# At most two indirect DMAs in flight, on two alternating semaphores

## What is computed

```python
# L0: two GCN layers of width 64 and 128
h = h @ W;  agg = segment_sum(h[src] * norm[:, None], dst);  out = agg + b
# L1: mean of the neighbours
aggregated = segment_sum(x[src], dst) / degree;  out = relu((aggregated + x) @ W.T + b)
# L2: five layers with edge attributes
m = relu(h[src] + edge_attr);  agg = segment_sum(m, dst);  z = h + agg   # then an MLP and batch norms
# L3: two layers of attention, 4 heads of 32
alpha = sum(q[dst] * (k[src] + e)) / sqrt(32);  w = softmax over the edges of one dst
out = segment_sum((v[src] + e) * w, dst) + x @ Ws + bs
```

## Time and profile before

| | us |
|---|---|
| median of 3 runs | 11942.19 |
| lowest, highest run | 11933.62, 11957.39 |
| span of the profiled execution | 11940.9 |
| POOL busy (share) | 5772.2 (48%) |
| PE busy (share) | 7779.4 (65%) |
| DVE busy, ACT busy | 5508.8, 4782.2 |
| L1960 gathers busy, 2682 and 894 | 2587.9, 861.3 |
| L1214 gathers busy, 1664 | 1651.9 |

### The profile page before, as it was taken

How to read it: one execution, slowest core, us unless ns; L and a number is a source line. 1 busy time by engine, 2 the same in 40 slices (tenths; PEclk the granted TensorE clock), 3 DMA queues, 4 the chain that set the end, 5 groups by cost and what they waited for, 6 DMA issues and landing times. The chain is left out here.

```text
span 11940.9 us, 256001 instructions
## 1 busy us (share of the span) xinstructions
PE 7779.4 (65%) x61807; PEld 6543.1 (55%) x61808; DVE 5508.8 (46%) x14938; ACT 4782.2 (40%) x13040; POOL 5772.2 (48%) x5856
## 2 busy tenths in 40 slices
PE   5357757767767776776777777677645555455555
PEld 3345535547746675665665667576444444344454
DVE  6545533333334444445445444444535456445447
ACT  0023323332324435444444443444445555345554
POOL 2455555554455444443443443444255555465554
PEclk6568878868878887888888888788766778667777
DMA  2235532233335544544554544455344454344453
GB/s 53 66 109 146 149 87 80 81 111 94 92 90 155 150 143 130 152 150 121 156 151 120 155 150 135 139 155 152 102 130 144 146 146 131 106 142 146 143 148 105
DMA packets 1224489, 1511.30 MB, mean 127 GB/s; under 512 B 206846, under 2 KB 806434, under 8 KB 1207895
## 3 DMA queue, kind: packets, MB, share of 16 engines
q1 hardware_dynamic: 1016374, 1055.75, 28.2%
q0 software_dynamic: 207712, 450.99, 14.9%
HBM read 1276.37 MB, written 229.67 MB: 126 GB/s over the span
## 5 line engine op out<-in xcount | busy, mean ns | idle before, releaser
L1960 POOL DMA_INDIRECT rings<-rows_key,pick x2682 | 2587.9, 965 | 3112.8 <-ACT pick L1975 2447.1
L2091 PE MATMUL wide<-bigDEF,bigC 128*128 128x128 bf16 (+2 forms) x32256 | 2353.5, 233 | 1289.3 <-issue 1239.5
L2091 PEld LDWEIGHTS wide<-bigDEF,bigC 128*128 128x128 bf16 x32256 | 2044.1, 110 | 1614.9 <-issue 1560.1
L1214 POOL DMA_INDIRECT bigDEF<-rows_key_value,idx x1664 | 1651.9, 993 | 1372.9 <-ACT idx L1226 742.8
L2202 DVE TENSOR_TENSOR bigDEF<-bigDEF,part 128x128 f32 (+1 forms) x3576 | 1016.7, 284 | 2643.3 <-PE part L2056 1435.5
L1975 ACT COPY pick<-pairs 128x3 int32 (+1 forms) x1192 | 222.5, 189 | 3794.2 <-PE part L2056 2957.9
L2056 PE MATMUL part<-rings 128*128 128x128 f32 (+1 forms) x7152 | 1283.6, 323 | 469.5 <-issue 231.4
L2056 PEld LDWEIGHTS part<-rings 128*128 128x128 f32 (+1 forms) x7152 | 1095.2, 213 | 565.8 <-issue 487.4
L1960 POOL DMA_INDIRECT rings<-rows_hidden,pick x894 | 861.3, 963 | 757.0 <-ACT pick L1975 535.3
L1330 PE MATMUL part<-bigB,rings 128*128 x3328 | 739.0, 390 | 730.4 <-DVE bigDEF L1417 363.6
L1982 ACT ACTIVATE rings<-iota,pairs 128x128 f32<-128x128 f32 x3576 | 1173.1, 391 | 47.8 <-remote 34.8
(11 more groups left out here) (424 smaller groups left out, 10607.0 us busy)
## 6 DMA issues: line engine op xcount, KB each, us to landing
bigC<-sheaf_hots SPq DMA_DIRECT2D x1152, 256.0 KB
rings<-in_attr SPq DMA_DIRECT2D x2235, 64.0 KB
bigC<-sheaf_attr SPq DMA_DIRECT2D x120, 1024.0 KB
walk_value<-bigDEF SPq DMA_DIRECT2D x416, 256.0 KB
rings<-walk_value SPq DMA_DIRECT2D x416, 256.0 KB
rings<-sheaf_steps SPq DMA_DIRECT2D x192, 256.0 KB
sheaf_hots<-bigC SPq DMA_DIRECT2D x192, 256.0 KB
bigB<-sheaf_hots SPq DMA_DIRECT2D x192, 256.0 KB
```

Of the source, the lines that this page charges most:

```text
L1214: e.indirect_dma_start(gbuf[:, g, r, :], None, table, bass.IndirectOffsetOnAxis(ap=c.idx[:, g, r:r + 1], axis=0)).then_inc(c.gathered[g].s ...
L1960: e.indirect_dma_start(gbuf[:, draw(n), r, 0:width], None, table, bass.IndirectOffsetOnAxis(ap=c.pick[:, draw(n), r:r + 1], axis=0)).then_ ...
L2091: last = e.matmul(to, hot, terms, start=x < LOT and x % batch == 0 and j == 2, stop=x >= MARCH - LOT, skip_group_check=True)
```

## The change

Every gather but the first two of a block waits until the second last gather has landed. For this the semaphores per buffer become two that alternate from gather to gather (`ALOFT` = 2; three in the first preparation, where three lists are fetched in turn). Whoever consumed a buffer now waits on both semaphores, up to the count at the end of its bunch or group. The first round of `_converse` on POOL is taken out of the loop. Nothing is computed differently, and no transfer is added or removed.

```diff
+ALOFT = 2
-    c.fetched = [gate(f"fetched{i}", 0) for i in range(SHELVES)]
+    c.fetched = [gate(f"fetched{i}", 0) for i in range(ALOFT)]
-    c.drawing = [gate(f"drawing{i}", 0) for i in range(DRAWS)]
+    c.drawing = [gate(f"drawing{i}", 0) for i in range(ALOFT)]
-    c.gathered = [gate(f"gathered{i}", 0) for i in range(RING)]
+    c.gathered = [gate(f"gathered{i}", 0) for i in range(3)]
...
+                    if k > 0:
+                        e.wait_ge(c.gathered[t].sem, c.gathered[t].at(16 * k))
                     e.indirect_dma_start(out, None, ins[src],
...
@@ _fetch
-        at = first + k * size + a
+        at, done = first + k * size + a, (k * size + a) // ALOFT
+        landing = c.fetched[a % ALOFT]
+        if done > 0:
+            e.wait_ge(landing.sem, landing.at(16 * done))
         e.indirect_dma_start(shelves[b][:, a, :], None, c.attr,
-                             bass.IndirectOffsetOnAxis(ap=c.edgeS[:, at:at + 1], axis=0)).then_inc(c.fetched[b].sem, 16)
+                             bass.IndirectOffsetOnAxis(ap=c.edgeS[:, at:at + 1], axis=0)).then_inc(landing.sem, 16)
@@ _stow
-        e.wait_ge(c.fetched[b].sem, c.fetched[b].at(16 * size * (use + 1)))
+        for landing in c.fetched:
+            e.wait_ge(landing.sem, landing.at(16 * size // ALOFT * (k + 1)))
@@ _converse, store on SP and multiply on DVE
-                e.wait_ge(c.gathered[g].sem, c.gathered[g].at(16 * GROUP * (i + 1)))
+                for landing in c.drawing:
+                    _hold(e, landing, 16 * GROUP // ALOFT * (i * RING + g + 1), c.tick_dve)
@@ _converse on POOL
-            with _loop(e, 0, ROUNDS) as i:
+            def fetch(i, g):
+                _hold(e, c.index, i * RING + g + 1, c.tick_pool)
+                for r in range(GROUP):
+                    landing, done = c.drawing[r % ALOFT], (i * RING + g) * (GROUP // ALOFT) + r // ALOFT
+                    if not (isinstance(done, int) and done == 0):
+                        _hold(e, landing, done * 16, c.tick_pool)
+                    e.indirect_dma_start(gbuf[:, g, r, :], None, table,
+                                         bass.IndirectOffsetOnAxis(ap=c.idx[:, g, r:r + 1], axis=0)
+                                         ).then_inc(landing.sem, 16)
+            for g in range(RING):
+                fetch(0, g)
+            with _loop(e, 1, ROUNDS) as i:
                 for g in range(RING):
-                    _hold(e, c.index, i * RING + g + 1, c.tick_pool)
-                    for r in range(GROUP):
-                        e.indirect_dma_start(gbuf[:, g, r, :], None, table,
-                                             bass.IndirectOffsetOnAxis(ap=c.idx[:, g, r:r + 1], axis=0)
-                                             ).then_inc(c.gathered[g].sem, 16)
+                    fetch(i, g)
@@ _mixed on POOL, inside fetch(i, n)
+                    t = (LEAD + n) * BUNCH + r
+                    landing, done = c.drawing[t % ALOFT], i * (BODY * BUNCH // ALOFT) + t // ALOFT
+                    if not (isinstance(done, int) and done == 0):
+                        _hold(e, landing, done * 16, c.tick_pool)
@@ _mixed, scatter on PE (sum); the same in join on DVE (edge)
-                    _hold(e, c.drawing[draw(n)], uses(i, n, DRAWS), c.tick_pe)
+                    for b, landing in enumerate(c.drawing):
+                        _hold(e, landing, landed(i, n, b), c.tick_pe)
```

23 lines of the change are left out of this document (15 added, 8 removed).

## The result

| | before | changed |
|---|---|---|
| median, us (4 runs each) | 11949.79 | 12346.12 |
| lowest, highest | 11933.62, 11959.39 | 12330.54, 12357.03 |
| span of the profiled execution | 11940.9 | 12328.7 |

The changed kernel takes 1.0332 times as long (95% interval 1.0316 to 1.0348). The forecast was 12300 us, between 11960 and 12600.

A forecast was written before the change was run, and what follows sets the result against it. It took POOL to have thin room, idling mostly for ACT's indices, and to become the bound in `_converse` under the limit. 312 + 46 + 65 + 15 + 20 - 100 = +358 on 11942 gave 12300 us, range 11960 to 12600.

The forecast's parts named there:

- `_converse`: Two passes of 832 gathers: 1.90 us a gather makes POOL the bound, 1581 us against 1425, +312 for both.
- The bound by the smallest row: In `_converse`: with SP's smallest row, 2.89 us, a pair takes 3.69 us and the stage 1535 us, +110 each time.
- the one by PE's 2.6: In `_converse`: with PE's 2.6 us a pair takes 3.4 us; only the first 48 groups lose, +46 for both.
- rival 2: Whole kernel: landings seen after 2.6 us, restart 0.3, 1.45 us a gather; only leads and fills pay; 11867 us, chance 0.14.
- The sums: Three "sum" passes at 1.70 us a gather: +30 for the first, +8 for each other, together +46.
- The edge layers: Five "edge" passes: the loop hides 1.70 of 1.95 us a gather, the lead doesn't; +13 a pass, +65.
- Second waits: At the consumers PE, DVE and SP: one more wait with a register each, +15, bounds 0 and 60.
- Preparation, units and fills: Preparation, the 4 units behind the sort block, fills behind passes: 0.2 us a gather, half hidden, +20.
- The sort block: A thinner gather stream lets PE keep its pace; block ends at 523 us in place of 638; -100 taken.
- Rival 1: Sort block: PE's slow pace stays, +29 in place of -100; 12430 us, chance 0.28.
- Rival 3: Late landings cost more than their mean: `_converse` about +560, "edge" layers some +20 each; about 12620 us, chance 0.12.
- Rival 4: Hardly more than two gathers in flight already, so only added waits count; 11942 to 11960 us, chance 0.06.

The follow-up runs named there:

- e3: Changed kernel with four semaphores in turn and four gathers in flight instead of two: 9243.07 us, 1.0321 times the kernel before in its set.
- e1: Kernel before with the limit of two only in `_fetch` and `_stow` (sort block, 4 units, fills): 9054.89 us, ratio 1.0109.
- e5: Kernel before, without an edit, traced at the free (faster) level: 8951.27 us in its one execution.
- e4: Kernel before with the limit of two only in `_mixed` (three sum and five edge passes): 11133.79 us, ratio 1.2432.
- e12: Kernel before with the limit of two only in the sort block and the 4 units behind it, held level: 11716.02 us, ratio 0.9971.
- e9: Changed kernel with POOL's side of `_converse` written out, all wait counts constant: 12065.25 us, 1.3466 times the kernel before.
- e11: Kernel before, no limit, a waited-for memset on POOL behind each gather of sort block and 4 units: 9012.89 us, ratio 1.0054.
- e6: Changed kernel, without an edit, at the free (faster) level: 12300.79 us, 1.3736 times the kernel before.
- e8: Kernel before, no limit, four semaphore increments behind each gather in `_fetch`, `_converse` and `_mixed`: 8961.39 us, ratio 0.9999.

## Why the prediction was right, point by point

**The sign and the size** hold at the level at which it was made. They don't hold in general: at the free level the same change costs 37%. The prediction read "room" out of 1.71 to 1.95 us a gather as what the stages need. That was the step with the hidden fault. Those figures were not the need of PE, ACT and DVE but the pace at which a hampered PE let POOL go; at the free level the same stages take a gather every 1.27 to 1.30 us, and POOL is the bound. The limit sets nearly the same absolute time at either level, so it cost little where the time was already lost.

**How near the total came was in good part luck.** The sum of 358 us met a measured 388, but the terms missed by far more than 30: the sum passes cost 90 us more than said, `_converse` 46 and the sort block 30, while the edge layers cost 58 less, preparation, units and fills together 52 less, what follows each `_converse` 11 less, and the 15 for second waits show nowhere. The misses add up to 166 us one way and 136 the other.

**`_converse`** (+312, measured +358): the mechanism as forecast. The windows are 1612 and 1604 us where 1581 was said; a pair takes 3.87 us, not 3.8. The bound by the smallest row, and the one by PE's 2.6, were both too low. The Trainium skill, page DMA: Bandwidth & Descriptors, section Anatomy of one DMA — SWDGE (gpsimd) path, led to an estimate of 2.3 us for such a gather; the packet records of the changed kernel give a median of 2.45 and a mean of 2.62 us from start to landing in that stage. So the trace is above it by little. What rival 2 missed is what follows the landing: until POOL starts the next gather, 3.87 - 2.62 = 1.25 us go by on average. The prediction also put the half busy DMA engines down to SP's transfers; in the second `_converse` of before the gathers' own queue has 27.6% of them and SP's 21.1%.

**The sums** (+46, measured +136 in the passes): here a term was mis-sized. The first pass took +156 where +30 was said. The 1.70 us a gather came from two rows of PE's waits in the lead; in the loop of that pass a landing takes 2.86 us in the mean and 1.40 go by behind it (packet records of the changed kernel), 2.13 us a gather, where the pass had one every 1.78 before. The prediction priced the pass without that pace of its own. In the second pass it is 2.30 and 1.30, so 1.80 us a gather and not 1.70. That used up all of the room under 1.81, and the pass lost nothing.

**The edge layers** (+65, measured +7 for the whole part): their windows grew by 10 to 17 us where 13 was said; two of the five are over the 15 that I had named as the bound of the test. The stretches between them got shorter by nearly as much. That the windows fit is luck: the rule allows a gather every 1.98 us there (landing 2.67, behind it 1.29) and not every 1.70, and POOL waits for landings 255.9 us in one layer, so it is the bound or close to it. This 1.98 happens to lie next to the 1.95 of before. At the held level the limit took PE's stalls away: 162.9 us of "issue" before L2091 in one layer before and 21.0 in the changed one, where PE's longest waits are for DVE (137.0 us). A gain that I had put in the sort block alone was at work here too.

**Second waits** (+15) can't be told apart. e3 has four such waits at each consumer, the same instructions on POOL and a limit of four, and all of this together costs 286 us at the free level, 29 of them in one `_converse`. No run prices the second waits alone, and none at the held level.

**Preparation, units and fills** (+20): preparation +17.7 and the 4 units +6.8 are more than the whole term; the stretches with fills gave 56.9 us back. The sign of the fills was wrong. The likely reason is that of the sort block: they are back-to-back streams beside PE's work too, and I had not carried the finding over. That is argued and not shown, for e1's rival, that the limit inside the passes shortens these stretches, was not tried at this level; at the free level they take 339 us in e5, 376 with the limit on the shelves alone (e1) and 319 with the limit in the passes alone (e4).

**The sort block** (-100, measured -70): that the limit ends PE's slow pace held. e12 at the held level shows PE's stall gone in the block where the limit stands and present in the loops where it doesn't. The condition that the prediction gave for it, a stream of one gather in 1.32 us, did not hold: at the held level PE has the stall in loops with one gather in 1.71 to 1.95 us too. The prediction had written that `_converse` shows no such stretch, but in its first 250 us DVE's L1412 waits 104.0 us for "remote", as DVE's L867 does in the sort block. The size was too large because the wait costs 1.69 us a gather and not 1.47. A landing takes 2.46 us in the mean and 0.93 go by behind it (packet records), 3.39 us a pair where 2.9 was said. Part of it are gathers that POOL itself writes for 1.5 to 2.8 us (30 of 192; 262.33 above). Why those take long was not tried; they are found where DVE is busy beside POOL, and of the last 52, from 500 us on with DVE standing still, none took more than 0.95. The block is bound by POOL at the end, with DVE idle for 90.3 us.

**Rivals.** Rival 1 (the slow pace stays) is out by the missing row. Rival 2 is out by e9 and the windows. Rival 3's 12620 did not come, though the landings of the first sum are its mechanism in small. Its own terms also add up to 12583 us, or to 12648 if its +20 a layer stand on top of the 13, and not to 12620. Rival 4 is out: POOL waits for landings 932.7 and 1550.8 us.

**Open.** What puts the kernel at one level or the other isn't known; no edit here touches it, and the same chip showed both. Why PE's instructions come late beside bunched gathers at that level isn't shown either. Whether PE's slow pace ends through a thinner stream or through the limit as such was meant to be told by e11, which ran at the free level where there is none; the edge layers say only that the mean pace alone isn't it. The level of e12's set was also not quite that of the first pair (11755 and 11950 for the same kernel).

## What to carry to other kernels

The idle time of an engine under a slow neighbour is not room: before a wait is put on it, ask whether the neighbour's pace is its own, above all where PE or DVE idles on "issue" or "remote" in an otherwise full stretch. Waiting for the landing of the gather before the last costs the landing plus 1.25 to 1.4 us a pair, which here is 1.8 to 2.1 us a gather in a loop, against 1.27 to 1.30 without where POOL is the bound; three in flight give some 70% of that back and four over 90%. And measure a change more than once on different occasions when the kernel's own time is not the same: this one was 3% slower and 37% slower.

## What the runs showed of the hardware

- The same program took 11950 and 8954 us, 1.33 times apart, each within 0.5% inside a set except the last (11672 to 11781). Beside gathers in bunches PE idles with nothing shown that it waits for at one level (3179 us before the matmuls of the sorted edges) and much less at the other (545 us), with transfers that land no sooner (2.75 and 2.87 us).
- Behind a wait for a landing with a register, inside a hardware loop, the next gather starts 1.25 us after the landing in the mean, behind one with a constant count 0.77 us (e6, e9); a pair gets 0.31 us shorter by it, as landings take 0.17 us longer.
- With at most two gathers in flight a landing of 128 KB takes 2.62 us in the mean, with three 2.95, with no limit at the same level 2.87 to 2.94.
- Four more semaphore increments behind each of some 5,600 gathers cost nothing (e8); a memset of 0.22 us with its wait makes the stream 0.22 us a gather slower, 1.60 in place of 1.38 (e11).
- At both levels POOL's writing of a gather takes the same, 965 and 977 ns.
